# An attention GNN kernel: the messages' weights stay in PSUM, in two banks, and the sums get two banks instead of three

## The reference

```python
for l in range(L):
    xn = _layernorm(h, ln1_g[l], ln1_b[l])
    q = (xn @ wq[l] + bq[l]).reshape(n, H, DH)
    k = (xn @ wk[l] + bk[l]).reshape(n, H, DH)
    v = (xn @ wv[l] + bv[l]).reshape(n, H, DH)
    scores = jnp.einsum('ehd,ehd->eh', q[dst], k[src]) * scale
    m = jax.ops.segment_max(scores, dst, num_segments=n)
    ex = jnp.exp(scores - m[dst])
    z = jax.ops.segment_sum(ex, dst, num_segments=n)
    attn = ex / z[dst]
    agg = jax.ops.segment_sum(attn[:, :, None] * v[src], dst, num_segments=n)
    ...
    h = h + ffn
```

## Time and profile before

| | |
|---|---|
| median of three runs | 4966.45 us (4961.32 to 4966.91) |
| the profiled execution | 4962.96 us |
| its span from the first to the last instruction | 4961.2 us |
| PE, DVE, ACT, POOL busy, share of the span | 77%, 73%, 44%, 69% |
| mean granted TensorE clock | 0.891 of full speed |
| edge phase of layer 0, of layer 1 | about 415 to 1630 us, about 2680 to 3890 us |

### The profile page before, as it was taken

The page is one execution under the profiler, slowest core; times in us unless marked ns, Lnnn a source line. Parts: engine busy times, 40 slices in busy tenths (PEclk is TensorE's granted clock), DMA queues, the critical chain, the costliest instruction groups (busy, mean ns, idle before and its releaser), DMA issues. The chain is left out here.

```text
span 4961.2 us, 83422 instructions
## 1 busy us (share of the span) xinstructions
PE 3805.9 (77%) x17590; PEld 2998.5 (60%) x17591; DVE 3606.3 (73%) x9840; ACT 2203.0 (44%) x5509; POOL 3436.7 (69%) x3005
## 2 busy tenths in 40 slices
PE   2597888888888677777677888888888677777759
PEld 1344666666666566666544666666666566666646
DVE  3587999999999644444377999999999744444458
ACT  0113666666666333333202666666666333333312
POOL 1215777777777288888823777777777288888857
PEclk9898899999999788888888889998999788888879
DMA  4356777777777366666635777777777366666668
GB/s 121 109 195 216 225 227 225 229 230 227 230 229 226 95 128 128 128 128 127 106 101 164 229 228 229 229 226 228 229 229 227 111 128 128 128 128 126 128 153 235
DMA packets 664219, 882.11 MB, mean 178 GB/s; under 512 B 126257, under 2 KB 492269, under 8 KB 664013
## 3 DMA queue, kind: packets, MB, share of 16 engines
q0 software_dynamic: 261248, 529.64, 44.0%
q1 hardware_dynamic: 369907, 322.55, 21.3%
q10 hardware_dynamic: 32860, 28.05, 1.9%
HBM read 749.33 MB, written 130.59 MB: 177 GB/s over the span
## 5 line engine op out<-in xcount | busy, mean ns | idle before, releaser
L793 POOL DMA_INDIRECT kv<-kv_scratch,src_u x1760 | 1856.6, 1055 | 544.5 <-issue 415.7
L1248 POOL DMA_INDIRECT sum_scratch<-ysum,dest x800 | 1257.5, 1572 | 243.3 <-issue 152.7
L1065 PE MATMUL sum_p<-msg,hot_s 128*128 128x273 f32 x3520 | 1041.5, 444 | 154.2 <-DVE msg L919 129.6
L1052 PE MATMUL qe<-sums,hot_q 128*128 x3520 | 902.5, 402 | 59.3 <-DVE prod L904 35.2
L1065 PEld LDWEIGHTS sum_p<-msg,hot_s 128*128 128x128 f32 x3520 | 725.4, 213 | 360.5 <-issue 193.8
L1052 PEld LDWEIGHTS qe<-sums,hot_q 128*128 128x128 f32 x3520 | 700.9, 203 | 217.1 <-issue 95.7
L904 DVE TENSOR_TENSOR prod<-qe,kv 128x1024 f32<-128x1024 f32 x440 | 536.5, 1219 | 141.5 <-DMA kv<-kv_scratch,src_u 116.9
L919 DVE TENSOR_TENSOR msg<-kv,W 128x1024 f32<-128x1024 f32 x440 | 535.7, 1217 | 40.2 <-issue 40.2
L824 ACT ACTIVATE hot_s<-iota_f,ndrel_u 128x128 f32<-128x128 f32 x1760 | 556.9, 390 | 13.7 <-PE sum_p L1065 7.0
L911 DVE TENSOR_REDUCE S<-prod 128x32 f32<-128x1024 f32 x440 | 534.8, 1215 | 0.6
L1487 PE MATMUL w_p<-xT,w_s 128*128 128x128 f32 x3200 | 471.4, 317 | 0.0
(11 more groups left out here) (233 smaller groups left out, 5264.7 us busy)
## 6 DMA issues: line engine op xcount, KB each, us to landing
drow<-drel_scratch SPq DMA_DIRECT2D x220, 256.0 KB
ea<-in_edge_attr SPq DMA_DIRECT2D x100, 512.0 KB, 5.3
srow<-in_src_rows SPq DMA_DIRECT2D x100, 512.0 KB, 5.3
kv<-kv_scratch,src_u POOLq DMA_INDIRECT x1760, 4.1
kv_scratch<-res SPq DMA_DIRECT2D x100, 256.0 KB, 2.0
hin<-h_scratch SPq DMA_DIRECT2D x154, 128.0 KB
h_scratch<-res SPq DMA_DIRECT2D x150, 128.0 KB, 1.7
masks<-mask_scratch SPq DMA_DIRECT2D x110, 128.2 KB
```

The source lines that it names most:

```text
L793: g.indirect_dma_start(out=kv[:, slot, :], out_offset=None, in_=KVd, in_offset=bass.IndirectOffsetOnAxis(ap=src_u[:, par, u:u + 1], axis=0 ...
L1052: ins = pe.matmul(qe[q % 2][:, i, u * D:(u + 1) * D], hot_q[:, q % 2, 2 * i + u, :], sums[:, bass.ds(tile * XW + XW, D)], start=True, stop ...
L1065: ins = pe.matmul(bank[:, 0:XW], hot_s[:, q % 2, 2 * i + u, :], msg[:, q % 2, 2 * i + u, :], start=(u == 0), stop=(u == 1))
L1248: g.indirect_dma_start(out=sum_d[r], out_offset=bass.IndirectOffsetOnAxis(ap=dest[:, k, j:j + 1], axis=0), in_=ysum[:, k, j, :], in_offset ...
```

## The change

The message's weights are read where PE left them, in `turned`, and not from the copy `W`. So `turned` has to stay until the messages of its batch are formed, and there are two banks of it, one for even and one for odd batches. The eighth bank comes from `sum_p`, which has two banks now, the first for the even pair of each step and the second for the odd one. The copy to `W` stays, for the columns that ACT puts beside the messages. The waits follow: the turning of the scores waits for the copy of two batches back and for the messages that read this bank, and the sum of a pair waits for the add just before instead of the one before that.

```diff
                 deltas = sb(ph, "deltas", [P, H])
                 scale = sb(ph, "scale", [P, H])
                 qe = [ph.enter_context(nc.psum_tensor(f"qe{j}_{l}", [P, 2, 512], f32)) for j in range(2)]
-                sum_p = [pb(ph, f"sum_p{j}") for j in range(RING)]
-                turned = pb(ph, "turned")
-                small = turned[:, 2 * P:2 * P + H]
+                sum_p = [pb(ph, f"sum_p{j}") for j in range(2)]
+                turned = [pb(ph, f"turned{b}") for b in range(2)]
 
                 s = Names(pool)
                 consts, dve_ready, pool_go, block_s = s.many(4)
...
                                     a.wait_ge(delta_s, n)
                                     a.wait_ge(shift_s, n)
                                     wait(a, rescaled, n * 2 - 2)
-                                    a.activation(scale[:, :], small, ACT.Exp).then_inc(scale_s, 1)
-                                    a.activation(ex[:, 0, :], turned[:, 0:P], ACT.Exp).then_inc(exp_s, 1)
+                                    a.activation(scale[:, :], turned[1 - par][:, 2 * P:2 * P + H], ACT.Exp).then_inc(scale_s, 1)
+                                    a.activation(ex[:, 0, :], turned[1 - par][:, 0:P], ACT.Exp).then_inc(exp_s, 1)
                                 if q == 2 and has_chain(n):
                                     a.wait_ge(wT_s, n)
                                     wait(a, msg_s, n * GQ - 2 * GQ)
                                     wait(a, wcopy_s, n * GQ - 2 * GQ)
-                                    a.activation(W[:, 1 - par, :, :].rearrange("p r u -> p (r u)"), turned[:, 0:2 * P],
+                                    a.activation(W[:, 1 - par, :, :].rearrange("p r u -> p (r u)"), turned[1 - par][:, 0:2 * P],
                                                  ACT.Copy).then_inc(w_s, 1)
                                 if q < 3 and has_message(n):
                                     hot_for_sums(n - 2, par, t, q + 1)
...
                             v.wait_ge(w_s, n - 1)
                             wait(v, sum_s, c * 2 - 2)
                             v.tensor_tensor(out=heads(msg[:, q % 2, :, 0:D]), in0=heads(kv[:, slot:slot + 4, D:2 * D]),
-                                            in1=W[:, par, 0:H, 4 * q:4 * q + 4].rearrange("p r u -> p u r")
+                                            in1=turned[par][:, 0:P].rearrange("p (r u) -> p u r", u=UB)[:, 4 * q:4 * q + 4, :]
                                             .unsqueeze(3).to_broadcast([P, 4, H, DH]), op=ALU.mult).then_inc(msg_s, 1)
 
-                        def add(c, bank, tile):
+                        def add(c, i, tile):
 
                             v.wait_ge(sum_s, c + 1)
                             wait(v, add_s, c)
                             at = sums[:, bass.ds(tile * XW, XW)]
-                            v.scalar_tensor_tensor(out=at, in0=at, scalar=keep[:, bass.ds(c, 1)], in1=sum_p[bank][:, 0:XW],
+                            v.scalar_tensor_tensor(out=at, in0=at, scalar=keep[:, bass.ds(c, 1)], in1=sum_p[i][:, 0:XW],
                                                    op0=ALU.mult, op1=ALU.add).then_inc(add_s, 1)
 
                         def step(i, k):
...
 
                             v.wait_ge(scT_s, n)
                             v.wait_ge(masks_in, n * 16)
-                            v.tensor_tensor_scan(run_l, masks[:, 0:P], turned[:, 0:P], begin[:, 2:3], ALU.add, ALU.max
+                            v.tensor_tensor_scan(run_l, masks[:, 0:P], turned[par][:, 0:P], begin[:, 2:3], ALU.add, ALU.max
                                                  ).then_inc(chain_s, 1)
-                            v.tensor_tensor_scan(run_r[:, ::-1], masks[:, 1:RW][:, ::-1], turned[:, 0:P][:, ::-1], -BIG,
+                            v.tensor_tensor_scan(run_r[:, ::-1], masks[:, 1:RW][:, ::-1], turned[par][:, 0:P][:, ::-1], -BIG,
                                                  ALU.add, ALU.max).then_inc(chain_s, 1)
                             v.wait_ge(chain_s, step(n, 2))
                             v.transpose(ends[:, :, :], runs[:, :, 0:BK]).then_inc(chain_s, 1)
...
 
                         def period(n, par, t, ring):
                             lo = n * GB - 2 * GB - DVE_AT
-                            bank = (ring + 1) * GB - DVE_AT
                             tiles = ()
                             if has_message(n) or has_message(n - 1):
                                 tiles = registers(DVE_E, nt_dve[0:1, bass.ds(n * GB - 2 * GB, GB)])
...
                                 if adds:
                                     if q == 1:
                                         v.wait_ge(rescaled, n * 2 - 2)
-                                    add(lo + 2 * q, (bank + 2 * q) % RING, tiles[2 * q])
+                                    add(lo + 2 * q, 0, tiles[2 * q])
                                 if has_scores(n):
                                     products(n, par, t, ring, q)
                                 if adds:
-                                    add(lo + 2 * q + 1, (bank + 2 * q + 1) % RING, tiles[2 * q + 1])
+                                    add(lo + 2 * q + 1, 1, tiles[2 * q + 1])
                                 if has_scores(n):
                                     scores(n, par, q)
                                 if q == 0 and has_message(n):
...
                                                     sums[:, bass.ds(tile * XW + XW, D)], start=True, stop=True)
                             ins.then_inc(q_s, 1)
 
-                        def sum_up(n, ring, q):
+                        def sum_up(n, q):
                             c = n * GQ - 2 * GQ + q
                             pe.wait_ge(hot_s_s, c + 1)
                             pe.wait_ge(wcopy_s, c + 1)
                             pe.wait_ge(msg_s, c + 1)
                             for i in range(2):
-                                bank = sum_p[((ring + 1) * GB + 2 * q + i) % RING]
-                                wait(pe, add_s, c * 2 + i - 2)
+                                wait(pe, add_s, c * 2 + i - 1)
                                 for u in range(2):
-                                    ins = pe.matmul(bank[:, 0:XW], hot_s[:, q % 2, 2 * i + u, :],
+                                    ins = pe.matmul(sum_p[i][:, 0:XW], hot_s[:, q % 2, 2 * i + u, :],
                                                     msg[:, q % 2, 2 * i + u, :], start=(u == 0), stop=(u == 1))
                                 ins.then_inc(sum_s, 1)
 
...
                             for q in range(GQ):
                                 if q == 0 and has_chain(n):
                                     pe.wait_ge(red_s, n * GQ)
-                                    wait(pe, w_s, n - 1)
-                                    pe.transpose(turned[:, 0:P], turn_scores(n, par), ident[:, :]).then_inc(scT_s, 1)
+                                    wait(pe, w_s, n - 2)
+                                    wait(pe, msg_s, n * GQ - 2 * GQ)
+                                    pe.transpose(turned[1 - par][:, 0:P], turn_scores(n, par), ident[:, :]).then_inc(scT_s, 1)
                                 if q + 1 < GQ and has_scores(n):
                                     spread(n, q + 1, tiles[2 * q:2 * q + 2])
                                 if q + 1 == GQ and has_scores(n + 1):
...
                                     if q == 1:
                                         pe.wait_ge(chain_s, n * CK - CK + 14)
                                         wait(pe, scale_s, n - 1)
-                                        pe.matmul(small, chain[:, 2 * BK:CW], deltas[:, :],
+                                        pe.matmul(turned[1 - par][:, 2 * P:2 * P + H], chain[:, 2 * BK:CW], deltas[:, :],
                                                   start=True, stop=True).then_inc(delta_s, 1)
-                                        pe.matmul(turned[:, 0:P], turn_scores(n, par), ident[:, :], start=True, stop=False)
+                                        pe.matmul(turned[1 - par][:, 0:P], turn_scores(n, par), ident[:, :], start=True, stop=False)
                                         pe.wait_ge(chain_s, n * CK - CK + 15)
-                                        pe.matmul(turned[:, 0:P], neg_ident[:, :], peak[:, :], start=False,
+                                        pe.matmul(turned[1 - par][:, 0:P], neg_ident[:, :], peak[:, :], start=False,
                                                   stop=True).then_inc(shift_s, 1)
                                 if q == 2 and has_chain(n):
                                     pe.wait_ge(scale_s, n)
                                     pe.wait_ge(exp_s, n)
                                     pe.wait_ge(chain_s, n * CK)
-                                    pe.transpose(turned[:, 0:P], ex[:, 0, :], ident[:, :])
-                                    pe.transpose(turned[:, P:2 * P], ex[:, 1, :], ident[:, :]).then_inc(wT_s, 1)
```

(4 more changed lines are left out.)

## The result

The changed kernel takes 4877.31 us (median of four, 4874.15 to 4881.06) against 4963.89 (4960.54 to 4966.91) before: ratio 0.9826, 95% interval 0.9809 to 0.9843. That is 87 us less; 86 were forecast, and 4880 us. A repeat on another chip gave 0.9822 (0.9805 to 0.9838). On two further chips the kernel before itself took 5554 and 5504 us; what was measured there is told with the experiments.

What follows compares the result with a forecast made beforehand. POOL, issuing gathers at 1.366 us each, was taken to bound the edge phase; -89 + 2 + 1 + 0 = -86 us from the median of 4966.4 gave 4880 us. The forecast's own range was 4867 to 4896, widened up to 4924.

Steps and rivals of the forecast that it cites:

- POOL sets the pace: Edge phase, main stretch: 16 gathers a batch x 1.366 = 21.9 us on POOL, against 20.42 for VectorE alone.
- -89 us of waits before the products: VectorE's waits before the products (line 904) in both layers' main stretch would go: -89.0 us.
- 2 left over: Allowance of 2 us for the thin margin between POOL's 20.15 and VectorE's 20.42 us a batch.
- the 18.9 us with other names: Part of the 89.0 us of waits before the products not put down to `kv`, but counted to the gathers too.
- +1 us for the PSUM operand: Message multiplication with weights from PSUM: +2 ns x 440 = +1 us.
- The half-rate bound: Message multiplication: PSUM operand read at half rate, +1.07 us for each of 440, +470 us, 5350; slow-side rival, chance 0.07.
- The errata table: Message multiplication, rival: 62 cycles more for a PSUM source, 65 ns a message, 28 us in all, 4908; chance 0.05.
- 0 for the second `turned` bank and the missing sum bank: PE's new waits, for messages two batches back and for the add just before, would cost 0.
- The cover named: Sums needed later and PE's 1.8 us a batch of waiting absorb delays; without it +79 us, 4959, rival chance 0.03.
- DMA can keep the pace: Gathers in the main stretch: 4% more speed makes 236 GB/s and DMA share 0.79, as already seen.
- The turns stay: VectorE's stops at the turn of its loop, once in six batches, stay: 30.8 us in layer 0.
- The size: Whole kernel: forecast gain of 86 us, to 4880 us; the forecast was given chance 0.71.

## Why the prediction was right, point by point

- *POOL sets the pace, because gathers inside messages take 1.40 us and not 0.95.* Right, and shown both ways: the operand put back brings the stretch and the time back, and an SBUF operand in the products moves the stretch there.
- *-89 us of waits before the products, 2 left over.* 87.4 went. The rest, 54.1, is before the main stretch, as said (about 52). That the 18.9 us with other names belonged to the gathers too is borne out: they went with the others.
- *+1 us for the PSUM operand.* Measured -3 ns a message, -1 us, and not clear of the spread: 1209 to 1214 ns in four runs with it, 1214 to 1217 without. The half-rate bound did not come up. The errata table in VectorE: DVE Perf Modes (the Trainium skill), section The TRN2 errata, with 62 cycles more for a PSUM source, has no counterpart here: 1214 ns with either operand, and 20.42 us a batch before and after. The rule of SBUF — State Buffer (the Trainium skill), section Who interferes with whom, that two SBUF inputs contend with GpSimd's reads, is borne out by the moved stretch, 1.35 us inside products and 0.95 inside messages.
- *0 for the second `turned` bank and the missing sum bank.* 4967.4 against 4967.6 us with the operand put back, and in the changed kernel itself PE does wait more, 233.7 us for adds, but VectorE waits only 1.5 us for sums in layer 0 and 6.3 in the run. The cover named (the sums have a step to spare) holds with two banks; with one it was gone, on the slower chip.
- *DMA can keep the pace.* 0.78 and 234 GB/s, landing time 4.1 us as before.
- *The turns stay.* Nearly: the 30.8 us of layer 0 became 35.8, a small loss that the sum did not have. Five turns fewer in each layer gave 38 us over both.
- *The size.* It came out within 1 us of the forecast gain. The mechanism is shown; so close a match is in part luck. The runs of one kernel spread over 7 us, and from the first message to the last the edge phase shrank by 37.8 us in layer 0 (1182.0 to 1144.2) and 51.6 in layer 1 (1180.3 to 1128.7), 89 together, while the two profiled executions differ by 84.
- *What the prediction did not see,* and no row of the kernel before could show, is the two slower chips, on which the same step, with twelve periods on both sides, costs 5.4%.

## What to carry to other kernels

An engine with fixed gaps between its instructions can be the bound at 77% busy: add the gap to each instruction before reading its busy share. Where GpSimd issues gathers, look in the timeline at which VectorE instruction each long one starts in; moving one of two SBUF operands to PSUM cost VectorE nothing here and freed the gathers. Measure such a change on more than one chip: here its sign was not the same on all. When the bound has moved, look again for what used to be covered, here the turns of the loop.

## What the runs showed of the hardware

- A gather's issue takes 0.95 us on POOL. If it starts inside a 1.22 us VectorE instruction with two SBUF operands, it ends 0.8 us after that instruction's end, so it takes 1.0 to 2.0 us, 1.35 to 1.40 on average in these kernels; VectorE's own time does not change (1214 to 1217 ns).
- A 128x1024 f32 multiplication takes 1209 to 1221 ns with both operands in SBUF or one in PSUM, also when the PSUM operand is repeated 32 times and then steps by 16 elements.
- A turn of the loop costs VectorE about 5.1 us in layer 0 and about 3.0 in layer 1 of the changed kernel.
- Chips differ: the same kernel took 4964 to 4968 us on some and 5504 and 5554 on two others, and on one of these two the kernel with the faster gathers took 5.4% more (5761.1 against 5466.7), not less.
- On the two slower chips VectorE stood over 3 us before 721 adds of eight traces; in 709 of them PE's matmul had ended over 3 us earlier by the trace.
